# Relational graph layer on one core: x made the stationary operand, 320 count columns moving

## The reference

```python
Xs = X[src]                                   # 400,000 x 128
m_data = Xs @ W_data.T + b_data
m_ctrl = Xs @ W_control.T + b_control
msg = where(edge_types == 0, m_data, m_ctrl)
agg = segment_sum(msg, dst, num_segments=12500)
out = relu(agg + (X @ W_self.T + b_self))
return layernorm(x + out)                     # over the features, eps 1e-5
```

## Time and profile before

| | |
|---|---|
| time, median of 3 runs | 2256.65 us (2256.22 to 2260.75) |
| span of the profiled execution | 2255.3 us |
| TensorE clock granted, mean | 0.988 of full speed |
| PE, weight loads | 2108.4 us (93%), 1866.0 us (83%) |
| DVE | 1193.7 us (53%) |
| ACT | 1412.6 us (63%) |
| POOL | 1540.4 us (68%) |

### The profile page before, as it was taken

How to read it: one execution, slowest core, us unless ns; L and a number is a source line. 1 busy time by engine, 2 the same in 40 slices (tenths; PEclk the granted TensorE clock), 3 DMA queues, 4 the chain that set the end, 5 groups by cost and what they waited for, 6 DMA issues and landing times.

```text
span 2255.3 us, 65825 instructions
## 1 busy us (share of the span) xinstructions
PE 2108.4 (93%) x26955; PEld 1866.0 (83%) x26955; DVE 1193.7 (53%) x3465; ACT 1412.6 (63%) x2452; POOL 1540.4 (68%) x1632
## 2 busy tenths in 40 slices
PE   2899999999999999999999999999999999999998
PEld 2788888888888888888888888888888888888887
DVE  7654555554555555545555555455455555554543
ACT  5566666666666666666666666666666666665664
POOL 6377767767767676677776776766767776766662
PEclk9999999999999999999999999999999999999999
DMA  7422222222222222122222221222122212221210
GB/s 212 107 61 62 60 59 57 62 56 61 57 58 59 59 58 60 53 61 57 61 57 56 60 60 52 61 58 59 54 59 57 60 55 59 59 60 54 59 55 25
DMA packets 110265, 140.75 MB, mean 62 GB/s; under 512 B 39165, under 2 KB 83100, under 8 KB 109962
## 3 DMA queue, kind: packets, MB, share of 16 engines
q0 software_dynamic: 52640, 107.91, 16.9%
q1 hardware_dynamic: 57322, 28.57, 4.7%
HBM read 127.33 MB, written 9.03 MB: 60 GB/s over the span
## 4 chain that ended last, share of the span: by engine, by line
PE 76%; DVE 7%; issue 5%; ACT 5%; DVEq 4%; SPq 1%; DMA 1%; POOL 0%; ACTq 0%; POOLq 0%
PE apply_ps L656 43%; PE build L638 13%; PE sum_ps L620 8%; ACT cnt L833 4%; DVEq L1127 4%; DVE acc L1133 2%; PE misc L706 2%; PE misc L665 2%; PE misc L684 1%; DVE hot_q L1100 1%; PE misc L709 1%; PE misc L708 1%; PE misc L707 1%; PE misc L671 1%; DMA key_dram<-x_u 1%
## 5 line engine op out<-in xcount | busy, mean ns | idle before, releaser
L555 POOL DMA_INDIRECT rows<-in_x,src_t x1570 | 1489.8, 949 | 644.1 <-issue 400.7
L833 ACT ACTIVATE cnt<-build 128x784 fp32r<-128x784 f32 x1568 | 1205.7, 823 | 750.2 <-PE build L638 726.6
L656 PE MATMUL apply_ps<-x,cnt 128*128 128x258 f32 x9604 | 1366.9, 292 | 18.1 <-DVE sd L1153 17.3
L656 PEld LDWEIGHTS apply_ps<-x,cnt 128*128 128x128 f32 x9604 | 1235.3, 193 | 51.6 <-issue 36.7
L1100 DVE TENSOR_TENSOR hot_q<-const_ps,key_pq 128x784 bf16<-128x784 bf16 x784 | 432.0, 556 | 84.8 <-PE build L638 72.5
L638 PE MATMUL build<-hot_q,hot_p 64*128 64x98 bf16 x12544 | 451.6, 208 | 23.4 <-ACT cnt L833 14.3
L638 PEld LDWEIGHTS build<-hot_q,hot_p 64*128 64x128 bf16 x12544 | 317.2, 95 | 148.8 <-ACT cnt L833 24.1
L1131 DVE TENSOR_TENSOR acc_deg<-misc,acc_deg 2x32 f32 x314 | 56.2, 179 | 534.9 <-PE misc L665 426.7
L1096 DVE TENSOR_TENSOR hot_p<-const_ps,key_pq 128x1024 bf16<-128x1024 bf16 x392 | 268.2, 684 | 88.2 <-PE build L638 74.0
L620 PE MATMUL sum_ps<-rows,hot 128*64 128x129 f32 x3140 | 211.9, 280 | 3.1 <-DMA rows<-in_x,src_t 3.1
L620 PEld LDWEIGHTS sum_ps<-rows,hot 128*64 128x64 f32 x3140 | 171.8, 137 | 18.1 <-DMA rows<-in_x,src_t 4.6
(11 more groups left out here) (174 smaller groups left out, 959.9 us busy)
## 6 DMA issues: line engine op xcount, KB each, us to landing
rows<-in_x,src_t POOLq DMA_INDIRECT x1570
cnt_raw<-in_x SPq DMA_DIRECT2D x13, 448.0 KB, 7.4
x_u<-in_x SPq DMA_DIRECT2D x48, 64.0 KB
out<-y_sb SPq DMA_DIRECT2D x48, 64.0 KB
key_dram<-x_u SPq DMA_DIRECT2D x16, 160.5 KB
x_u<-in_x SPq DMA_DIRECT2D x36, 53.5 KB
out<-y_sb SPq DMA_DIRECT2D x36, 53.5 KB
win_i<-in_dst SPq DMA_DIRECT2D x25, 64.0 KB
```

The lines of the kernel that those rows point to most:

```text
L555: pool.indirect_dma_start(out=rows[:, slot, 0:D], out_offset=None, in_=x, in_offset=bass.IndirectOffsetOnAxis(ap=src_t[:, col:col + 1], ax ...
L656: last = pe.matmul(apply_ps[:, 0:ROW + 2], cnt[:, half, i, :], x2[:, b, :], start=(b == 0), stop=(b == XBLOCKS - 1))
L833: act.activation(o, i.rearrange("p h (m b) -> p b h m", b=HALF), ACT.Copy).then_inc(evacuated, 1)
```

## The change

- `x2` becomes the stationary operand of `apply`, in its high and its low part apart, and the counts move: 320 columns, which are 160 nodes x 2 types. Per 160 nodes there are 98 x 2 matmuls, 7840 in all instead of 9604. The sums come out with the features on the partitions, so `post`, `turn_block` and `take_block` go. DVE copies the 320 columns from PSUM to `fin` instead (`take_fin`, 40 times).
- The dense range is 6400 nodes in 40 groups of 160. A pass over one half takes 10 steps (`TURNS`), so there are 800 batches. A step holds one portion of apply, now 8 or 10 matmuls, ahead of its build, and apply runs 10 steps behind.
- `cnt` holds one half of a group in 49 rows of 320; the second half of a group is stored turned, in 10 runs of 32 columns, so that a slot is overwritten as soon as it was applied.
- `hot_p` is built in each batch (8 slots); `hot_q` has 8 slots instead of 12. One-hots are made two steps ahead instead of three.
- The degrees come from the keys: `prepare_keys` counts them in five more DVE operations, `turn_keys` turns them in two more matmuls, and three 16-bit parts of the biases (`bias9`) replace the 32-bit bias product of a dense unit.
- 154 rounds of gathers instead of 157, two rounds in 10 steps, still in five portions. `hot`, `sg` and `zg` have one buffer instead of two. In `add_sums` both loads of the window's place stand ahead of the wait for the sums; in DVE's step the one-hots now stand ahead of `add_sums` and the units.
- 60 dense units (128, 128, 64 nodes) instead of 49. x is loaded by ACT's queue straight into `x2`; one more copy of the first two chunks of keys is stored for the early groups.

```diff
-            def apply(y, c):
...
-                for i in range(b0, b1):
-                    b = half * HALF + i
-                    last = pe.matmul(apply_ps[:, 0:ROW + 2], cnt[:, half, i, :], x2[:, b, :],
-                                     start=(b == 0), stop=(b == XBLOCKS - 1))
-                if c == 4:
-                    last.then_inc(applied, 1)
+            def apply(a):
+
+                t, r = divmod(a, TURNS)
+                G, half = divmod(t, 2)
+                blocks = [half * HALF + q for q in dense_rows(r, half)]
+                if r == 0:
+                    pe.wait_ge(evacuated, 2 * TURNS * (t + 1))
+                    if half == 0 and G:
+                        pe.wait_ge(fin_taken, G)
...
+                for b in blocks:
+                    for k in range(2):
+                        last = pe.matmul(sums, x2[:, b, D * k:D * k + D], counts(b - half * HALF, half),
...
+                last.then_inc(applied, 1)
...
+            def take_fin(G):
+
+                dve.wait_ge(applied, 2 * TURNS * (G + 1))
+                dve.tensor_copy(fin[:, :, GROUP * (G % 2):GROUP * (G % 2) + GROUP],
+                                apply_ps[:, 0:COLS].rearrange("p (n t) -> p t n", t=2)).then_inc(fin_taken, 1)
...
             def add_sums(ps):
 
                 e = ps // EPOCH
+                bases = [dve.value_load(off_i[:, 2 * ps + g:2 * ps + g + 1], min_val=0, max_val=SPAN - WIN)
+                         for g in range(2)]
                 dve.wait_ge(misc_full, job[sum_step[ps]] + 1)
-                for g in range(2):
-                    base = dve.value_load(off_i[:, 2 * ps + g:2 * ps + g + 1], min_val=0, max_val=SPAN - WIN)
+                for g, base in enumerate(bases):
...
             for s in range(STEPS):
-                for c in split_at(s):
-                    split_lo(c)
-                if posted_at(s) is not None:
-                    post(posted_at(s))
+                if s in fin_at:
+                    take_fin(fin_at[s])
+                if batch_at(s + 2) is not None:
+                    make_onehots(s + 2)
+                if split_at(s) is not None:
+                    split_lo(split_at(s))
                 if sums_at(s) is not None:
                     add_sums(sums_at(s))
...
-                if batch_at(s + 3) is not None:
-                    make_onehots(batch_at(s + 3))
```

More of the change, by code:

```diff
@@ L115, in gnn_resnorm @@
         else:
-            u = v.n0 // P
-            assert v.out < block_step[min(2 * u + 4, BLOCKS - 1)]
+            assert v.out < fin_step(v.n0 // GROUP + 2), v
+            assert v.out < key_step.get(v.n0 // (4 * BLOCK) + DEG_RING, BATCHES + TURNS)
     TURN_END = BATCHES + 3
-    STEPS = max(taken) + 4
+    STEPS = max(max(taken) + 4, BATCHES + TURNS)
+    assert max(v.out for v in units) < BATCHES + TURNS
     gather_at = {s: r for r, s in enumerate(gather_step)}
@@ L430, in _ @@
             load_window(0)
-            for c in range(3):
-                load_xs(c)
+            for b in range(1, len(LISTS)):
+                load_lists(b)
             for k, w in enumerate((w_self, w_data, w_ctrl)):
@@ L619, in gather_sums @@
                     part, st = slice(64 * g, 64 * g + 64), g * GT + j
-                    last = pe.matmul(sum_ps[part, 0:D + 1], hot[:, ps % 2, st, :], rows[:, slot, 0:D + 1],
+                    last = pe.matmul(sum_ps[part, 0:D + 1], hot[:, st, :], rows[:, slot, 0:D + 1],
                                      start=(j == 0), stop=(j == GT - 1))
@@ L676, in turn_keys @@
                 pe.transpose(misc[:, 0:P], key_n[:, 0, :, :].rearrange("p h e -> p (h e)"), ident[:, :])
-                pe.transpose(misc[:, P:2 * P], key_n[:, 1, :, :].rearrange("p h e -> p (h e)"), ident[:, :]
-                             ).then_inc(misc_full, 1)
+                pe.transpose(misc[:, P:2 * P], key_n[:, 1, :, :].rearrange("p h e -> p (h e)"), ident[:, :])
+                for h in range(2):
+                    last = pe.matmul(misc[0:9, 2 * P + P * h:3 * P + P * h], deg_c[:, h, :], ident16[:, :],
+                                     start=True, stop=True)
+                last.then_inc(misc_full, 1)
             def turn_x(i):
@@ L713, in _ @@
             for s in range(STEPS):
-                y, c = divmod(s - APPLY_AT, 4)
-                if c == 0 and 0 < y <= 2 * BLOCKS:
-                    apply(y - 1, 4)
+                if apply_at(s) is not None:
+                    apply(apply_at(s))
                 if batch_at(s) is not None:
@@ L864, in normalise @@
                                ).then_inc(out_ready, 1)
+            for c in range(XCH):
+                load_x(c)
             store_lists(0)
@@ L1021, in _ @@
             step(dve.tensor_copy(part_f[:, :], part_i[:, :]))
+            step(dve.scalar_tensor_tensor(out=part_f[:, 4:5], in0=part_f[:, 5:6], scalar=-3.0,
+                                          in1=part_f[:, 0:1], op0=ALU.mult, op1=ALU.add))
+            for k in range(3):
+                dve.tensor_single_scalar(pick9[:, k:k + 1], part_f[:, 4:5], float(k), ALU.is_equal)
             step(dve.scalar_tensor_tensor(out=ptr[:, 0, 0:1], in0=part_f[:, 0:1], scalar=2.0,
@@ L1093, in make_onehots @@
+                dve.tensor_copy(deg_c[:, :, 3:6], ctrl)
+                dve.tensor_tensor(deg_c[:, :, 0:3], both, ctrl, ALU.subtract).then_inc(keys_ready, 1)
+            def make_onehots(n):
+                nb = TURNS * (n // (2 * TURNS)) + n % TURNS
+                half, s = n // TURNS % 2, 4 * (n % 2)
+                g, q = nb // 16, 8 * (nb % 16)
+                if n >= 2:
+                    dve.wait_ge(built, 2 * (n - 1))
+                if half == 0 and nb % 16 == 0:
                     dve.wait_ge(misc_free, key_job(g) + 1)
@@ new lines, in split_bias @@
+            def split_bias():
+                dve.wait_ge(bias9_loaded, 48)
+                step(dve.tensor_copy(b9_h, b9_f))
+                dve.tensor_scalar(bias9[:, :], b9_h, pick9[0:9, 0:1], None, ALU.mult)
+                step(dve.tensor_tensor(b9_f, b9_f, b9_h, ALU.subtract))
+                for k in (1, 2):
+                    step(dve.tensor_copy(b9_h, b9_f))
+                    last = dve.scalar_tensor_tensor(out=bias9[:, :], in0=b9_h, scalar=pick9[0:9, k:k + 1],
+                                                    in1=bias9[:, :], op0=ALU.mult, op1=ALU.add)
+                    if k == 1:
+                        step(dve.tensor_tensor(b9_f, b9_f, b9_h, ALU.subtract))
+                last.then_inc(bias9_ready, 1)
```

526 lines of the change are left out of this document (266 added, 260 removed).

## The result

The changed kernel takes 2252.08 us (2250.61 to 2255.78, 9 runs), the kernel before 2257.29 (2255.65 to 2262.82, 9 runs) beside it: ratio 0.9971, 95% interval 0.9960 to 0.9981. It is faster by 5 us; the forecast was 2269, slower by 12.

What follows compares the result with a forecast made beforehand. PE's own work was taken to bound the kernel, and within it apply. The terms summed to +21 us, less 9 for dependent waits: +12 on 2255.3, with 1.35 around it 2269 us; range 2207 to 2302, the forecast's own 2252 to 2286.

Steps and rivals of the forecast that it cites:

- Apply: PE's apply matmuls: 7840 of 320 columns at 146 ns replace 9604 at 120 ns, a gain of 8 us.
- A: Rival on apply: runs of ten at 145 ns a matmul where the forecast had 155; 2221 us, chance 0.22.
- Rival B: Apply's cost is in proportion to columns, 149 ns, or the turned half reads slower; 2292 us, chance 0.18.
- More of DVE's work: DVE's one-hots and other additions: 1482 us busy, beside PE's work; one-hots make PE wait +4, up to +30.
- Rival C: DVE sets the pace, late by 0.05 us more in each of 800 steps; 2309 us, chance 0.10.
- Blocks: The 98 turnings of blocks on PE go: 20 us of work and 20 of waits, a gain of 40.
- Waits for `misc`: PE's waits for the tile misc: +15 us against 24.4 before, between -15 and +50; near 40 in the new profile.
- Keys: Five more DVE operations at each group of keys, 1.2 us together; PE's waits +24, between +15 and +60.
- Start: First apply after ten steps instead of four, 30 us instead of 16, at about 70; +8, between -5 and +20.
- the forecast's own sign: If PE's waits together stay under 70 us, the forecast is wrong from its second term.
- the discount of 9: Taken off the 47 us of waits and fin, since the waits are not independent.
- Rival D: PE's waits for keys and misc stay at 61 us, apply as forecast; 2239 us, faster, chance 0.12.

Runs made afterwards that it cites:

- group 2: Follow-up runs sharing one chip, the kernel before at 2659 us; the changed kernel took 2732.1 there, ratio 1.0282.
- group 4: Follow-up runs sharing one chip, the kernel before at about 2259 us; the changed kernel took 2251.1 there, ratio 0.9963.
- groups 1 to 3: Follow-up runs, each group sharing a chip, in which the kernel before took 2701, 2659 and 2657 us.
- a_changed: The changed kernel run again unaltered, on a chip where the kernel before took 2659 us: 2732.1 us, ratio 1.0282.
- after: The changed kernel as first measured and profiled beside the kernel before: 2252.08 us, ratio 0.9971.
- e11_before_hotp: The kernel before with DVE building hot_p in every batch instead of every second: 2660.3 us, ratio 1.0014.
- e9_no_blocks: The kernel before without PE's turning of its 98 blocks and ACT's copies of them: 2654.8 us, ratio 0.9991.
- group 3: Follow-up runs sharing one chip, on which the kernel before took 2657 us.
- e5_cols: The changed kernel with apply's matmuls over 256 columns in the first half and 192 in the turned half: 2769.5 us, one run.
- e13b_sp_keys: The changed kernel with x loaded by SP and keys prepared a step earlier: 2196.7 us, 0.9723 of the kernel before.

## Why the prediction was wrong

*Apply: right.* 147 ns measured, 146 taken; by it the term is -10 instead of -8. No run shows the shorter matmul at 320 columns on which A's 2221 in the chances and its 145 among the signs rest: the part beyond the columns' time was 13.5 ns at 258 columns and 13.7 at 320, and the run of ten shown above has 159 with the run's start, where the forecast had 155. So A falls. Rival B's 149 is 2 ns off, but a cost in proportion would be 118 at 256 columns, where 120 was measured.

*More of DVE's work: right.* 1474.8 busy (1482), and nearly free where it was tried. Rival C falls on that count.

*Blocks: a little too large.* -33 instead of -40.

*Waits for `misc`: the step that failed.* "Now both loads are ahead of the wait, which shortens this by about 0.7, but DVE first makes one-hots", and so +15 against 24.4. Both halves of the step fail in the changed kernel on a chip like the first. The loads shorten next to nothing (2.36 to 2.30), since DVE comes to them behind the one-hots. The one-hots lengthen nothing, since they fill time in which DVE had been idle: the forecast took DVE as late at the additions, while its own row has it waiting 3.06 us for PE's sums, with the first load behind that wait. In the whole kernel before DVE idles 426.7 us ahead of L1131 until PE has turned sums; in the changed kernel there is no such wait. The forecast put the new end of the additions at about 1.24 + 1.0; it is 2.30 after PE's turning, where it was 2.36 before, so no reason for +15 was left. The waits for `misc`, step by step, in us:

| kernel | waits for `misc` |
|---|---|
| before | 27.8 |
| before, no block jobs | 15.5 |
| changed, loads back | 13.4 |
| changed | 7.1 |

Most of the fall is L670's own wait of 11.4, which the forecast had booked with the blocks; its "near 40" for the new profile counts it twice. Against what is left the term is -8 instead of +15.

*Keys: the work right, the wait too large.* From L1127 to the end of L1140 DVE takes 1.97 at a group of keys, where L1079 to L1083 took 0.94 (medians of 25): 1.03 more, 1.2 taken. But PE's wait rises by 6.3 and not by 24. The place loads have no part in that (40.6 with them put back). The new order of DVE has some: in group 2 the wait is 49.8 with the additions first and 42.2 with the one-hots first. What else takes up the five operations is open. By the forecast's own sign (PE's waits together under 70; they are 50) it is wrong from this second term on.

*Start: mis-sized.* The first apply was put at about 70 and comes at 86.8. The ten steps take 35.7 (30 taken), and the first build is 10.7 late, which had no term: I did not count that 14 loads were now issued by ACT ahead of its first copy, though the order of its instructions shows them there. With x loaded by SP the ten steps take 29.4 (35.2 to 64.6).

*A portion's wait for the last copy*: 14.8 us, not foreseen. I looked at take_fin there (0.7 us) and not at `evacuated`, the semaphore that tells of ACT's copies.

The two waits were put 41 us too high, 32 after the discount of 9; the start and the last copies were too low. That the total is off by only 17 is in part luck.

The parts don't add up either. In group 4 the loads alone are worth -50 in the kernel before, and all the rest on top of them +42 (2209.2 to 2251.1). In the other order the rest alone is worth -4 (2255.4 against 2259.5) and the loads on top -4. The old order of DVE's work can use the early loads and the new one can't: the additions end 1.34, 2.30 and 2.36 after PE's turning in the kernel before with its loads ahead, the changed kernel and the changed kernel with its loads back. Pace and start, with the pace as the time between the starts of apply's 393rd and 7743rd matmul, 600 steps of the old kernel and 750 of the new:

| kernel | steps | us a step | first apply |
|---|---|---|---|
| before | 784 | 2.765 | 56.3 |
| before, loads ahead | 784 | 2.706 | 55.7 |
| changed, loads back (group 4) | 800 | 2.689 | 86.2 |
| changed (group 4) | 800 | 2.680 | 86.5 |
| changed, x by SP, keys earlier | 800 | 2.639 | 64.6 |

Against the second row the changed kernel has 16 x 2.680 = 43 more for its batches and gets 784 x 0.026 = 20 back, +22; the start is 31 later; the remaining -11 was not broken down. Rival D is nearest in sign and number (waits shrink, 2239) and right about the 98 jobs; the loads did little of it, and it missed the start.

## What to carry to other kernels

A load of a register between a wait and the work that others wait for can be on the path, though the profile counts it nowhere as busy (in the kernel before, the additions ended 2.36 us after PE's turning with such loads and 1.34 with them moved ahead): look for idle time inside a group of instructions. Ahead of the wait it is free only if the engine really waits there; behind other work it costs the same as before (50 us in one order of work, 4 in the other). So ask first whether an engine that seems late is late or idle: work put into idle time can be nearly free (238 us more of DVE's here cost 3.6, in an interval of -2 to +10). Before a change of layout is priced, split off each small edit that comes with it and try it on the old kernel too: here one was worth 50 us, and the whole change 5 to 8. And look at what an engine issues ahead of its first work: here 14 transfers held ACT for 32 us.

## What the runs showed of the hardware

**Signals of PE that come late.** On the chips of groups 1 to 3 all kernels that also ran on the others take 18 to 22% longer (the changed one 2732.1 us against 2251.1). DVE's instructions take as long (1472.3 us busy in the changed kernel in group 2, `a_changed`, and 1474.8 on the first chip, `after`). PE is busy for 160 us more (2268.4 and 2108.6), at a granted clock of 0.945 against 0.980; the other two thirds of the 478 us between the two spans (2731.7 and 2254.0) are idle time of PE. The changed kernel in group 2, one build and who was waiting for it:
```profile
1222.02 0.56 PE L692 MATMUL build<-hot_q,hot_p 64*128 64x98 bf16 x16
...
1223.78 0.69 DVE L1152 TENSOR_TENSOR hot_p<-const_ps,key_pq 128x1024 bf16<-128x1024 bf16 x1 [1.72 <-PE build L692]
1223.78 0.83 ACT L883 ACTIVATE cnt<-build 128x784 fp32r<-128x784 f32 x1 [0.47 <-PE build L692]
1224.01 0.95 POOL L609 DMA_INDIRECT rows<-in_x,src_t  x1 [0.82 <-PE build L692]
```
```profile
PE build L692 <- ACT cnt L883: 215.3, 276, 8.0
```
The build ends at 1222.58, and three engines that wait for it start 1.2 to 1.4 us later, together. The changed kernel on the first chip, a build and DVE, which waits for it:
```profile
1010.23 0.55 PE L692 MATMUL build<-hot_q,hot_p 64*128 64x98 bf16 x16
```
```profile
1010.83 0.69 DVE L1152 TENSOR_TENSOR hot_p<-const_ps,key_pq 128x1024 bf16<-128x1024 bf16 x1 [0.99 <-PE build L692]
```
Here the build ends at 1010.78 and DVE starts 0.05 later. Counted from the start of a build's last matmul, over every hot_p ahead of which DVE had been idle since before that start, the records of `after` have a median of 0.25 us (451 of them; 99% under 0.33), those of `a_changed` one of 0.65 (344; one in ten over 2.3). Of the late starts in `a_changed` (over 0.5) 78% fell in a gather on POOL, of the prompt ones (under 0.3) 23%; but in `after` 70% of the prompt ones fell in one too, so a gather alone does not delay them. From the end of ACT's copy to PE's next work that waits for it the median is 0.053 us in `after` and 0.055 in `a_changed`. The wait of PE's builds for ACT's copy grows from 6.5 us (`after`) to 215 (`a_changed`), and it is there that the changed kernel looks more exposed (85 and 108 in two relatives of the kernel before, `e11_before_hotp` and `e9_no_blocks` in group 3). Why it is, and what delays the signals, stays open.

**A floor under short matmuls.** In `e5_cols` 192 columns came every 113 ns at the full clock and every 213 at half of it. Neither is the time of the columns (80 and 160, by the 0.83 ns a column at half the clock, above), while 256 columns at half the clock, 213 too, are just their own time. A limit is left that nearly doubles with half the clock. What sets it was not shown; that it is the load of the stationary columns would be a guess, since apply has 128 of them in every run.

**Issuing can cost more than it seems.** In `after` ACT was held 31.96 us for 14 loads of x (13 of 448 KB, one of 384 KB), 2.3 us each. SP, in the rows of the start above (`e13b_sp_keys`), issued a single load of 54 KB in 0.43, but 10 of x in a row in 16.4.

So loads in a row cost more than the first ones: of ACT's 14 the first three took 0.45 to 0.58 each to issue, the other eleven 1.42 to 4.76. The 2.3 us on average add up to 32 us in which ACT did nothing else (its first own instruction starts at 32.74), and moving them, with SP's new order, gave 25 us of the kernel (2732.1 to 2707.3, group 2).
